# An attention and expert kernel: TensorE takes the contexts of two units back directly behind the masks, ahead of the small products and the unit's transposes

## What is computed

```python
x = x + attention(layernorm(x), Wq, Wk, Wv, Wo)   # softmax(q k^T / sqrt(8), causal) v, then Wo
x = x + experts(layernorm(x), gate_w, w1, w2)     # softmax gate, top 64 tokens of each expert, gelu
```

## Time and profile before

| | |
|---|---|
| median of three runs | 558.08 us |
| the profiled execution, its own time | 557.51 us |
| its span, first to last instruction | 555.8 us |
| TensorE busy (matmuls) | 525.8 us, 95% |
| TensorE's weight loads, beside the matmuls | 426.6 us, 77% |
| VectorE busy | 416.0 us, 75% |
| ScalarE busy | 405.1 us, 73% |
| GpSimd busy | 253.6 us, 46% |
| granted TensorE clock, mean | 0.997 |

### The profile page before, as it was taken

How to read it: one execution, slowest core, us unless ns; L and a number is a source line. 1 busy time by engine, 2 the same in 40 slices (tenths; PEclk the granted TensorE clock), 3 DMA queues, 4 the chain that set the end, 5 groups by cost and what they waited for, 6 DMA issues and landing times.

```text
span 555.8 us, 13959 instructions
## 1 busy us (share of the span) xinstructions
PE 525.8 (95%) x4777; PEld 426.6 (77%) x4777; DVE 416.0 (75%) x1066; ACT 405.1 (73%) x1383; POOL 253.6 (46%) x249
## 2 busy tenths in 40 slices
PE   1489999999999999999999999999999999999996
PEld 1257777777777777778777777777689989999995
DVE  1477888888888888888898998899973876442354
ACT  4699989889888888889889898889655434334330
POOL 5165565565555655565464555457820111011011
PEclk9989999999999999999999999999999999999999
DMA  4577152731633325142250423501200011000011
GB/s 123 151 186 196 39 151 63 243 115 39 173 105 102 90 61 151 38 113 77 77 153 20 133 77 77 140 14 43 92 21 1 2 40 59 20 21 11 11 29 49
DMA packets 49783, 45.97 MB, mean 83 GB/s; under 512 B 4288, under 2 KB 46528, under 8 KB 49728
## 3 DMA queue, kind: packets, MB, share of 16 engines
q1 hardware_dynamic: 48864, 44.60, 29.2%
q10 hardware_dynamic: 864, 0.66, 0.4%
HBM read 26.35 MB, written 18.89 MB: 81 GB/s over the span
## 4 chain that ended last, share of the span: by engine, by line
PE 86%; DVE 5%; ACT 5%; DMA 2%; issue 2%; ACTq 0%; POOL 0%; DVEq 0%
PE ctx_ps L1075 15%; PE misc_ps L1084 11%; PE t_ps L1162 10%; PE t_ps L1048 6%; PE s_ps L1189 5%; PE t_ps L1049 5%; PE t_ps L1058 4%; PE misc_ps L1034 3%; PE s_ps L1146 3%; PE misc_ps L1036 3%; PE misc_ps L1035 3%; ACT prob L529 3%; PE s_ps L1276 2%; PE s_ps L1147 2%; PE s_ps L1148 2%; PE ctx_ps L1172 2%
## 5 line engine op out<-in xcount | busy, mean ns | idle before, releaser
L529 ACT ACTIVATE prob<-s_ps,neg_max 128x128 f32<-128x128 f32 (+1 forms) x512 | 209.6, 436 | 20.6 <-DVE neg_max L939 17.5
L489 POOL TENSOR_TENSOR probn<-prob,inv 128x1024 f32<-128x1024 f32 x64 | 121.2, 1893 | 55.3 <-DVE inv L960 55.3
L529 ACT ACTIVATION_READ_ACCUMULATOR prob<-s_ps,neg_max 128x1 f32 x512 | 113.6, 222 | 0.0
L482 POOL TENSOR_TENSOR probn<-prob,inv 128x512 f32<-128x512 f32 x64 | 66.5, 1040 | 74.6 <-PE t_ps L1058 66.8
L883 DVE TENSOR_REDUCE neg_max<-s_ps 128x4 f32<-128x1024 f32 x64 | 76.3, 1193 | 1.1 <-PE s_ps L1194 1.1
L1084 PE MATMUL misc_ps<-wo_sb,ctxT 128*128 128x128 f32 x512 | 73.9, 287 | 0.7 <-DVE x_all L708 0.7
L506 POOL TENSOR_TENSOR y_parts<-y_sb,y_parts 128x512 fp32r<-128x512 f32 x16 | 20.6, 1286 | 112.9 <-ACT y_parts L587 112.9
L1084 PEld LDWEIGHTS misc_ps<-wo_sb,ctxT 128*128 128x128 f32 x512 | 62.0, 191 | 11.4 <-issue 11.4
L577 ACT ACTIVATE hT<-s_ps 128x512 f32<-128x512 f32 x64 | 38.0, 596 | 44.7 <-PE s_ps L1148 42.2
L1048 PE MATMUL t_ps<-ident,probn 128*128 128x128 f32 x256 | 63.7, 289 | 0.8 <-ACT probT L543 0.7
L1049 PE MATMUL t_ps<-ident,probn 128*128 128x128 f32 x256 | 60.2, 275 | 0.0
(11 more groups left out here) (176 smaller groups left out, 1155.2 us busy)
## 6 DMA issues: line engine op xcount, KB each, us to landing
qT<-q_rows SPq DMA_DIRECT2D x15, 512.0 KB, 4.0
q_rows<-qk_hi SPq DMA_DIRECT2D x32, 128.0 KB, 2.4
q_rows<-qk_lo SPq DMA_DIRECT2D x32, 128.0 KB, 2.4
k_diag_odd<-k_rows SPq DMA_DIRECT2D x32, 128.0 KB, 4.2
k_rows<-qk_hi SPq DMA_DIRECT2D x30, 128.0 KB, 2.4
k_rows<-qk_lo SPq DMA_DIRECT2D x30, 128.0 KB, 2.4
k_diag_even<-k_rows SPq DMA_DIRECT2D x28, 128.0 KB, 4.2
w_raw<-in_L_ffn_w SPq DMA_DIRECT2D x1, 2048.0 KB, 9.3
```

The source lines that it names most:

```text
L482: nc.gpsimd.tensor_tensor(probn[r][:, 0:HG * P].rearrange("p (i k) -> p i k", i=HG), prob[r][:, 0:HG * P].rearrange("p (i k) -> p i k", i=HG),
L489: nc.gpsimd.tensor_tensor(probn[r][:, HG * P:].rearrange("p (i k) -> p i k", i=HG), prob[r][:, HG * P:].rearrange("p (i k) -> p i k", i=HG ...
L529: last = nc.scalar.activation(prob[r][:, first + i * keys:first + (i + 1) * keys], scores[:, i, :], ACT.Exp, bias=neg_max[:, r, block_, i: ...
```

## The change

In TensorE's `batch` the call of `contexts(u-2)` moves from behind the small step to directly behind the masks. The small steps of j=0, 2 and 3 move with it ahead of `turn(u-1)`, and `turn(u-1)` stands behind them. The small step of j=1 stays where it is in the text, now behind `turn(u-1)`. The order of steps is then: scores, masks, contexts, small step (j=0, 2, 3), turn, small step (j=1), project, turn_last, values, scores. No instruction is added or removed, all waits stay with the step that they belong to, and the other engines' programs are unchanged.

```diff
                         last.then_inc(s1_done, 1)
-                    if has(u - 1, UNITS):
-                        turn(u - 1, rm)
+                    if has(u - 2, UNITS):
+                        w, g = u - 2, (j - 2) % G
+                        vb = par if j >= 2 else 1 - par
+                        contexts(w, g, vb, r2)
+                    if j == 2 and has(b + 2, B):
+                        pe.wait_ge(xn1_ready, b + 3)
+                        await_count(pe, v_ready, u + 2)
+                        for tb in range(TB):
+                            last = nc.tensor.transpose(misc_ps[0][:, tb * P:(tb + 1) * P], xn1[:, tb, :], ident[:, :])
+                        last.then_inc(xT_done, 1)
                     if j == 3 and has(b + 2, B):
...
                         gate(b - 3, misc_ps[0])
                         if at(u, (44,)):
                             turn_probs(0, misc_ps[0][0:HALF, T:2 * T])
+                    if has(u - 1, UNITS):
+                        turn(u - 1, rm)
                     if j == 1 and has(b - 2, B):
...
                         turn_norms(b - 2, misc_ps[0])
-                    if j == 2 and has(b + 2, B):
-                        pe.wait_ge(xn1_ready, b + 3)
-                        await_count(pe, v_ready, u + 2)
-                        for tb in range(TB):
-                            last = nc.tensor.transpose(misc_ps[0][:, tb * P:(tb + 1) * P], xn1[:, tb, :], ident[:, :])
-                        last.then_inc(xT_done, 1)
-                    if has(u - 2, UNITS):
-                        w, g = u - 2, (j - 2) % G
-                        vb = par if j >= 2 else 1 - par
-                        contexts(w, g, vb, r2)
                     if has(u - 3, UNITS):
```

## The result

The kernel after takes 550.21 us, the median of four runs (548.63 to 551.22), against 558.28 us of the kernel before on the same chips (558.05 to 559.54). The ratio is 0.9852, with a 95% interval of 0.9836 to 0.9867: 8.1 us faster. The profiled execution took 549.33 us with a span of 547.6 us, 8.2 us less than before. Forecast were 548.2 us and a gain of 9.9 us.

What follows compares the result with a forecast made beforehand. TensorE's stream was taken to bound iterations 3 to 57; gains of 3.2, 2.5 and 4.2 us sum to 9.9, single iterations to 0. From 557.5 to 547.6 us, plus 0.57 for the median: 548.2 us, range 542.5 to 556.5.

Steps and rivals of the forecast that it cites:

- What bounds the kernel: TensorE's own stream sets iterations 3 to 57, busy for all of the 310.13 us from 48.87 to 359 us.
- Contexts' entry: Switch from masks' row halves into column halves costs 0.14 us as today: change 0, ends +0.14 or -0.15 us.
- Rivals B and C: New switch from masks into contexts costs 0.29 us: 556.4 us, 12%; or costs nothing: 540.5 us, 5%.
- Projection and turn: Projection 0.20 us less per iteration; turn's first transpose 0.15 us less behind a small step, otherwise no change.
- Rival F: Projection's extra 0.20 us comes from its weights or inputs, not the switch, and stays: 558 us, 5%.
- Small step: Directly behind the contexts it costs more: 0.16 us at j=2, 0.19 us at j=0 and j=3.
- What could be late: Contexts keep 0.68 us to VectorE's copy, so no wait; the later turn, which ScalarE awaits, is the tight place.
- ScalarE's path: From turn through ScalarE's copy and exponentials to the next scores: 0.12 us left at j=2, 0.34 us at j=1.
- Rival D: ScalarE's work from turn to next scores becomes the bound: 551 to 560 us; 12%, 7% of it slower than before.
- Single iterations: Iteration 2 loses 0.3 to 0.4 us, 43 loses 0.16, 58 to 62 gain nothing, 63 gains 0.5; together 0.
- rival E: Contexts wait for VectorE's copy in units with extra VectorE work (45 on): 13 iterations by 0.3 us, 552 us, 6%.

Runs made afterwards that it cites:

- Experiment 4: The kernel before with one more tiny ScalarE activation per iteration, between the copy of the turn's first half and the lower exponentials: 558.33 us, ratio 1.0003.
- experiment 7: The kernel before with its hardware loop (sequences 4 to 9) written out, so every wait compares with a constant: 557.70 us, ratio 0.9995.
- experiments 6 and 8: The kernel after, first with the hardware loop written out: 549.32 us; then with the loop kept and late waits put last on TensorE and ScalarE: 550.81 us.

## Why the prediction was right, and where it was off

*What bounds the kernel.* Right. TensorE alone made the iterations 3 to 57 before. Experiment 4 lengthened ScalarE's work, experiment 7 turned the loop's waits into waits for constants, and not one iteration from 3 to 57 moved by more than 0.02 us.

*Contexts' entry* (0 us, ends +0.14 and -0.15). Right, to 0.01 us: 1.45 us behind the masks. Rivals B and C are out. The choice of 0.14 us between the ends was an argument from the neighbouring prices, and it held. The statement of the Trainium skill, page TensorEngine Tiling (Array Packing), section Key Properties, that a change of mode drains the engine, fits this: the traces show one price of about 0.15 us for rows to columns, not the two of its ends. No row shows the drain itself.

*Projection and turn.* Right: 0.89 us, and 0.11 or 0.26 us for the first transpose. Rival F is out.

*Small step.* Right in itself at j=2 (0.37 us) and at j=3 (0.20 us of switch). At j=0 the gate's 0.54 us was right, and the step behind it was mis-sized. I let the turn's first transpose cost 0.11 us behind full-array work; behind the gate it costs 0.16. 12 x 0.05 = 0.6 us. The likely reason is that four products of 8 columns are too short to cover the next weights; no run varied their length, so it stays an inference from the two rows behind the gate.

*What could be late.* This is where the other 0.7 us of j=0 went. The prediction counted the margin of the contexts against VectorE's copy (0.68 us; right) but took that as the latest of their inputs, as it was before. With the later turn ScalarE's second copy moved from about 0.3 us ahead of the iteration's start to 0.44 us behind it and became the latest. ScalarE's loop was worked out only as far as the exponentials, not to the copy behind them. Even so the copy comes in time, 0.1 us ahead of the masks' end. It costs time only in the loop, at j=0, and there no longer once its wait stands behind the three others (experiments 6 and 8).

*ScalarE's path* (0.12 us left). Near enough: about 0.08 us outside the loop at j=3, more than 0.09 us at j=2, none in the loop at j=3. Rival D did not decide but stands next to it.

*Single iterations.* Iteration 2 lost 0.42 us for 0.3 to 0.4 expected. Iteration 43 kept its 6.38 us, as stated. Iteration 63 gave 0.8 us with what follows it, between 0 and 1.1 as stated. Iteration 61 was missed: there the contexts waited for VectorE, whose 0.1 us "issue" ahead of them stands at 375.47 us in this chain of the kernel after.

```profile
374.26 0.60 DVE ctxT L747
374.86 0.61 DVE probT L753
375.47 0.09 issue
375.56 1.52 PE ctx_ps L1075 x16
```

That is rival E in one iteration, 0.39 us. Iterations 58 and 60 gained 0.23 us, and 59 lost 0.12.

## What to carry to other kernels

When TensorE bounds a kernel, count how often its stream changes between full array, row halves and column halves, and group the steps so that the count falls; read the price off the chain by comparing the same step behind different neighbours. Before moving a step, list for each wait which input comes last after the move, not which came last before it, and follow the other engines' path to its end. In a hardware loop, try putting the wait that is released last behind the others: it gave 0.6 us in the iterations here, though not a measurable difference in the total.

## What was not expected of the hardware

- Four changes of the array's division were priced, and each costs 0.14 to 0.20 us: rows to full, full to columns, columns to full, and rows to columns (0.14 us). Only the step behind it matters a little: about 0.15 us ahead of transposes and contexts, 0.19 to 0.20 ahead of the projection, the gate and the query/key products. Full to rows, which the change left alone, was not priced.
- Behind the gate's four products of 8 columns the next transpose costs 0.16 instead of 0.11 us and the projection 0.99 instead of 0.89.
- In the hardware loop at j=0, a copy that ended 0.1 us ahead of its use still delayed the use by up to 0.17 us, with three waits on register values behind the wait for it. With constants, or with that wait last, the delay is gone. At j=1 of the same loop it did not appear.
